# Two reorderings in a four-layer kernel: the choice of experts ahead of the first shared product, and another order in the head and period of the fused loop

## The reference, cut to what matters

```
L0 attention: 16 heads, 4 kv heads, rope, causal softmax
L0 experts:   scores = softmax(t @ gate_w.T); top 2 of 16 experts (inner width 176), weighted
              y = sum of w_e * (silu(t@w1) * (t@w3)) @ w2;  z = the same with the shared weights (width 352)
L1 ssm:       zxbcdt = x @ W_in; causal conv over 4 taps, silu; dt = softplus(dt + bias); dA = exp(dt * A)
              h = h*dA + dt*x*B;  y = h.C + D*x;  y = y * silu(gate)
              y = y * rsqrt(mean(y*y) + eps) * norm_w;  out = y @ W_out
L1 experts:   sigmoid scores, top 8 of 16 (width 128), normalised, scale 2.5, plus 2 shared experts
```

## Time and profile before

| what | value |
|---|---|
| median of 3 runs | 1957.74 us |
| lowest and highest | 1949.46, 1965.22 us |
| the profiled execution, its run | 1958.08 us |
| its span, first to last instruction | 1956.4 us |
| TensorE busy (matmuls) | 1837.6 us, 94% |
| VectorE busy | 1265.4 us, 65% |
| ScalarE busy | 768.6 us, 39% |
| GpSimd busy | 424.6 us, 22% |
| mean granted TensorE clock | 0.962 of full |

### The profile page before, as it was taken

How to read it: one execution, slowest core, us unless ns; L and a number is a source line. 1 busy time by engine, 2 the same in 40 slices (tenths; PEclk the granted TensorE clock), 3 DMA queues, 4 the chain that set the end, 5 groups by cost and what they waited for, 6 DMA issues and landing times.

```text
span 1956.4 us, 33621 instructions
## 1 busy us (share of the span) xinstructions
PE 1837.6 (94%) x9986; PEld 1417.0 (72%) x9987; DVE 1265.4 (65%) x3638; ACT 768.6 (39%) x1483; POOL 424.6 (22%) x708
## 2 busy tenths in 40 slices
PE   5999999969989999777999999999999999999998
PEld 3566666547766666555888888888888888888886
DVE  3577677545432222377777877887787778777843
ACT  1466666543223333343433343344333433433321
POOL 1244334331854444300110010011001100110000
PEclk9899999879989999887999999999999999999999
DMA  9900000001332333342112201220222022112210
GB/s 357 223 6 1 0 0 1 1 1 39 116 106 92 92 94 95 118 155 81 49 39 87 82 28 64 87 81 6 87 87 75 12 86 82 52 40 71 66 49 11
DMA packets 92119, 137.87 MB, mean 70 GB/s; under 512 B 18548, under 2 KB 76148, under 8 KB 91508
## 3 DMA queue, kind: packets, MB, share of 16 engines
q1 hardware_dynamic: 85108, 117.83, 18.9%
q0 software_dynamic: 6912, 18.92, 2.7%
HBM read 98.51 MB, written 38.22 MB: 70 GB/s over the span
## 4 chain that ended last, share of the span: by engine, by line
PE 43%; issue 38%; DVE 8%; POOL 7%; ACT 2%; DMA 1%; DVEq 0%; SPq 0%; POOLq 0%; ACTq 0%
PE bank L610 6%; PE bank L184 5%; PE bank L1311 4%; PE bank L631 4%; POOL sorted_in L858 3%; PE bank L1376 3%; PE bank L1269 2%; PE bank L193 2%; PE bank L1317 2%; PE bank L1299 2%; PE bank L1404 2%; PE bank L621 1%; PE bank L1362 1%; PE bank L539 1%; PE bank L1279 1%
## 5 line engine op out<-in xcount | busy, mean ns | idle before, releaser
L184 PE MATMUL bank<-moe_xT,up_w 128*128 128x256 f32 x2304 | 547.9, 381 | 0.0
L184 PEld LDWEIGHTS bank<-moe_xT,up_w 128*128 128x128 f32 x2304 | 439.8, 191 | 60.5 <-issue 0.2
L227 ACT ACTIVATE moe_silu<-bank 128x256 f32<-128x256 f32 x288 | 110.8, 385 | 576.3 <-PE bank L184 576.3
L193 PE MATMUL bank<-down_w,moe_hT 128*128 128x256 f32 x1152 | 303.9, 387 | 5.7 <-DVE moe_hT L294 2.9
L193 PEld LDWEIGHTS bank<-down_w,moe_hT 128*128 128x128 f32 x1152 | 207.1, 190 | 39.2 <-DVE moe_hT L294 8.2
L1557 DVE TENSOR_REDUCE q_slots<-bank 128x4 f32<-128x1024 f32 (+1 forms) x96 | 117.7, 1226 | 82.1 <-PE bank L1311 81.6
L1462 ACT ACTIVATE probs<-bank 128x1024 f32<-128x1024 f32 x96 | 98.2, 1023 | 100.6 <-PE bank L1317 100.6
L830 DVE TENSOR_TENSOR moe_h<-moe_silu,bank 128x176 f32<-128x176 f32 x80 | 27.0, 338 | 140.2 <-issue 83.2
L610 PE MATMUL bank<-up_w,moe_xT 128*128 x320 | 116.8, 488 | 0.7 <-ACT moe_xT L676 0.6
L1311 PE MATMUL bank<-kT,qT 16*128 16x256 f32 (+1 forms) x1024 | 115.2, 353 | 0.0
L293 DVE TENSOR_TENSOR moe_silu<-moe_silu,up_w 128x256 f32<-128x256 f32 x192 | 81.2, 423 | 51.7 <-ACT moe_silu L227 42.3
(11 more groups left out here) (309 smaller groups left out, 3257.9 us busy)
## 6 DMA issues: line engine op xcount, KB each, us to landing
up_w<-comb_rows SPq DMA_DIRECT2D x32, 768.0 KB, 5.2
m<-decay_rows SPq DMA_DIRECT2D x16, 1024.0 KB, 5.0
comb_got<-results SPq DMA_DIRECT2D x16, 768.0 KB, 7.7
moe_rows<-sorted_in SPq DMA_DIRECT2D x80, 128.5 KB
sorted_in<-zero SPq DMA_DIRECT2D x10, 1024.0 KB, 10.0
down_w<-comb_rows SPq DMA_DIRECT2D x16, 512.0 KB, 8.5
up_w<-in_up SPq DMA_DIRECT2D x2, 3168.0 KB, 15.2
up_w<-in_up SPq DMA_DIRECT2D x2, 2304.0 KB, 12.0
```

The lines of the kernel that those rows point to most:

```text
L184: last = mm(k.bank[:, UP_BANK + i % 3, half * S:(half + 1) * S], m.w_up[:, c, at + half * m.inter:at + (half + 1) * m.inter], m.xT[:, par, ...
L193: last = mm(k.bank[:, SUM_BANK, j * D:(j + 1) * D], m.hT[:, i % 3, j * P:(j + 1) * P], m.w_down[:, m.expert(i), :], start=(i == 0 and j == ...
L227: nc.scalar.activation(m.silu[:, i % 3, :], k.bank[:, UP_BANK + i % 3, 0:S], ACT.Silu).then_inc(m.silu_ready, 1)
```

## The change

**Shared stage.** Piece 0 of the choice goes ahead of the first transposes, pieces 1 to 3 ahead of the first up product, the others each some places earlier (piece 14 stays); the two rank products go from (1, 1) and (2, 1) to (0, 2) and (1, 2). The scatters start at (2, 2) instead of (3, 0).

**Scaling of `w_out`.** It moves from the start of the fused loop to VectorE's queue right behind the last shared step.

**Late steps.** ScalarE's Silu is cut from `l_up` as a step of its own, `l_silu`. In the head, for sequence b, the up products go behind `turn_dt`, the Silus behind the decays, the products `l_h` behind conv 2 and conv 3; `turn_dA`, `decay_out`, `decay_in` go ahead of the gates.

**Period.** In `THEN`, `table` 0, `one_plus`, `table` 1, `conv` 3 and `dt` 1 of the next sequence go from step 8 to step 9, behind `post` 0; step 8 keeps `out` and `conv` 2.

```diff
@@ -386,17 +386,21 @@
 
 
 CHOSEN = 12
-CHOICE = {(0, 0): (0,), (0, 1): (1, 2, 3), (0, 2): (4, 5, 6, 7), (1, 2): (8, 9), (2, 0): (10,), (2, 2): (11, 12), (3, 0): (13,),
-          (4, 0): (14,)}
-RANKS = {(1, 1): 0, (2, 1): 1}
-SCATTERS_FROM = 3
+AT_ONCE = (1, 2, 3)
+CHOICE = {(0, 0): (4, 5), (0, 1): (6, 7), (1, 0): (8,), (1, 1): (9, 10), (2, 0): (11, 12), (2, 1): (13,), (4, 0): (14,)}
+RANKS = {(0, 2): 0, (1, 2): 1}
+SCATTERS_FROM = (2, 2)
 EARLY = 14
 
 
 def shared_steps(chunks):
     yield "norm", 0, 0
+    yield "choose", 0, 0
     yield "turn_x", 0, 0
-    places = chunks * (EARLY - SCATTERS_FROM)
+    for n in AT_ONCE:
+        yield "choose", n, 0
+    first = chunks * SCATTERS_FROM[0] + SCATTERS_FROM[1]
+    places = chunks * EARLY - first
     tile = 0
     for t in range(EARLY):
         for c in range(chunks):
@@ -411,7 +415,7 @@
                 yield "turn_x", t + 1, 0
             for n in CHOICE.get((t, c), ()):
                 yield "choose", n, 0
-            place = chunks * (t - SCATTERS_FROM) + c + 1
+            place = chunks * t + c + 1 - first
             while place > 0 and tile < -(-TILES * place // places):
                 yield "scatter", tile, 0
                 tile += 1
@@ -817,6 +821,7 @@
     for what in shared_steps(m.shared_chunks):
         shared(*what)
 
+    scale_w_out(k, m.ssm, dve)
     seen = [0]
 
     def block(what, b, row):
@@ -903,7 +908,7 @@
     go_through(m.blocks, sp, block)
 
 
-LATE_STEPS = ("l_norm", "l_turn", "l_up", "l_h", "l_down", "l_end")
+LATE_STEPS = ("l_norm", "l_turn", "l_up", "l_silu", "l_h", "l_down", "l_end")
 
 
 class Late:
@@ -966,7 +971,7 @@
         if what == "l_turn":
             act.wait_ge(s.xT_full, m.turns + n + 1)
             nc.scalar.copy(moe.xT[:, t % 2].rearrange("p c t -> p (c t)"), k.bank[:, SUM_BANK, :]).then_inc(s.xT_ready, 1)
-        if what == "l_up":
+        if what == "l_silu":
             w = s.wide(c)
             act.wait_ge(s.up_full, m.up(t, c) + 1)
             if n > 0:
@@ -2027,6 +2032,13 @@
     return step
 
 
+def scale_w_out(k, m, dve):
+    dve.wait_ge(m.loaded, m.LOADS)
+    for f in range(FT):
+        last = k.nc.vector.tensor_scalar(m.w_out[:, f, :], m.w_out[:, f, :], m.norm_w[:, f:f + 1], None, ALU.mult)
+    last.then_inc(m.w_out_ready, 1)
+
+
 def ssm_vector(k, m, combine, dve, chain):
     nc = k.nc
     v = nc.vector
@@ -2160,10 +2172,6 @@
     link(v.memset(m.feat_bc[:, 0:TAPS - 1], 0.0))
     dve.wait_ge(m.loaded, m.LOADS)
 
-    for f in range(FT):
-        last = ts(m.w_out[:, f, :], m.w_out[:, f, :], m.norm_w[:, f:f + 1], None, ALU.mult)
-    last.then_inc(m.w_out_ready, 1)
-
     ts(m.a_lim[:], m.a_log[:], 88.0, None, ALU.min).then_inc(m.log_ready, 1)
     dve.wait_ge(m.tables, 2)
     link(ts(m.neg_a[:], m.pos_a[:], -1.0, None, ALU.mult))
@@ -2310,8 +2318,8 @@
         ((1, "turn_dt", 0), (0, "ymm", 1), (0, "square", 0), (1, "dt", 0), (1, "conv", 0), (-2, "m_post", 1)),
         ((1, "gate", 0), (0, "gating", 1), (2, "c_sum", 0)),
         ((1, "gate", 1), (0, "square", 1), (1, "conv", 1), (-2, "store", 0)),
-        ((0, "out", 0), (1, "table", 0), (1, "one_plus", 0), (1, "table", 1), (1, "conv", 2), (1, "dt", 1), (1, "conv", 3)),
-        ((0, "post", 0),),
+        ((0, "out", 0), (1, "conv", 2)),
+        ((0, "post", 0), (1, "table", 0), (1, "one_plus", 0), (1, "table", 1), (1, "conv", 3), (1, "dt", 1)),
         ((0, "post", 1), (1, "silu", 0), (2, "c_sum", 1)),
         ((1, "turn_c", 0), (0, "m_norm", 0)),
         ((1, "turn_c", 1), (0, "m_norm", 1), (1, "dt", 2), (2, "c_norm", 0)),
@@ -2339,15 +2347,16 @@
     def head(self):
         a, b = range(EARLY, B)
         yield "c_fetch", 0, 0, 0
-        for what, t, i in (("l_norm", a, 0), ("l_turn", a, 0), ("l_up", a, 0), ("c_sum", 0, 0), ("l_up", a, 1), ("c_sum", 0, 1),
-                           ("l_up", a, 2), ("l_h", a, 0), ("c_norm", 0, 0), ("l_h", a, 1), ("c_fetch", 1, 0),
-                           ("experts", 0, 0), ("norm", 0, 0), ("l_h", a, 2), ("l_norm", b, 0), ("norm", 0, 1),
-                           ("l_down", a, 0), ("turn_x", 0, 0), ("l_turn", b, 0), ("feat", 0, 0), ("l_up", b, 0), ("feat", 0, 1),
-                           ("l_h", b, 0), ("l_up", b, 1), ("bcdt", 0, 0), ("l_h", b, 1), ("turn_dt", 0, 0),
-                           ("dt", 0, 0), ("table", 0, 0), ("conv", 0, 0), ("one_plus", 0, 0), ("table", 0, 1), ("l_up", b, 2),
+        for what, t, i in (("l_norm", a, 0), ("l_turn", a, 0), ("l_up", a, 0), ("l_silu", a, 0), ("c_sum", 0, 0), ("l_up", a, 1),
+                           ("l_silu", a, 1), ("c_sum", 0, 1), ("l_up", a, 2), ("l_silu", a, 2), ("l_h", a, 0), ("c_norm", 0, 0),
+                           ("l_h", a, 1), ("c_fetch", 1, 0), ("experts", 0, 0), ("norm", 0, 0), ("l_h", a, 2), ("l_norm", b, 0),
+                           ("norm", 0, 1), ("l_down", a, 0), ("turn_x", 0, 0), ("l_turn", b, 0), ("feat", 0, 0), ("feat", 0, 1),
+                           ("bcdt", 0, 0), ("turn_dt", 0, 0), ("l_up", b, 0), ("l_up", b, 1), ("l_up", b, 2),
+                           ("dt", 0, 0), ("table", 0, 0), ("conv", 0, 0), ("one_plus", 0, 0), ("table", 0, 1),
                            ("dt", 0, 1), ("conv", 0, 1), ("dt", 0, 2), ("table", 0, 2),
-                           ("gate", 0, 0), ("conv", 0, 2), ("gate", 0, 1), ("turn_dA", 0, 0), ("decay_out", 0, 0), ("l_h", b, 2), ("conv", 0, 3),
-                           ("silu", 0, 0), ("decay_in", 0, 0), ("l_down", b, 0), ("c_sum", 1, 0), ("c_sum", 1, 1),
+                           ("turn_dA", 0, 0), ("decay_out", 0, 0), ("decay_in", 0, 0), ("l_silu", b, 0), ("l_silu", b, 1),
+                           ("gate", 0, 0), ("conv", 0, 2), ("l_silu", b, 2), ("l_h", b, 0), ("gate", 0, 1), ("conv", 0, 3),
+                           ("l_h", b, 1), ("silu", 0, 0), ("l_h", b, 2), ("c_sum", 1, 0), ("l_down", b, 0), ("c_sum", 1, 1),
                            ("c_norm", 1, 0), ("turn_c", 0, 0), ("turn_c", 0, 1),
                            ("norm", 1, 0), ("norm", 1, 1), ("turn_x", 1, 0), ("xdt", 0, 0)):
             yield what, t, t % 2, i
@@ -2474,6 +2483,7 @@
         comb_rows = nc.dram_tensor("comb_rows", (2, E, S), F32, kind="Internal").ap()
         second = Moe(k, 128, 2.5, up_w, down_w, gate1, [(moe1_loaded, 80)], comb_rows)
         attention, tail = Attention(k, a, gate0, first), Tail(k, Combine(k, results), Ssm(k, a), second, Late(k, first, second))
+        first.ssm = tail.ssm
         layers = [attention, first, tail]
         tail.weights(sb)
 
```

## The result

The changed kernel took 1983.89 us (median of 6 runs, 1980.3 to 1994.3), the kernel before 1956.55 us beside it: ratio 1.0137, 95% interval 1.0109 to 1.0164, so 27 us slower (21 to 32). Timed again later beside other runs of before it was 1978.40 against 1960.61 us, 1.0096 (1.0073 to 1.0118). Both intervals lie on the slower side; their middle is +23 us. The forecast was 1980.4 us.

A forecast was written before the change was run, and what follows sets the result against it. TensorE was taken to bound the loop's full periods (940.0 of 946 us busy), GpSimd the shared stage. 30.4 - 4.0 - 1.2 - 0.55 - 1.95 = +22.7 us gave 1980.4 us; own range 1973 to 1988, 8 in 10 1964 to 1999.

The forecast's parts named there:

- The size of the stall: Full periods: ScalarE's table detour behind step 9's Silu delays TensorE's `turn_c` by 2.17 us, 14 times, 30.4 us.
- the 0.48 us that TensorE waited for product 10 is not given back: Full periods: TensorE's 0.48 us wait stays despite the stall, since VectorE's own order moves by as much.
- My lower bound: Full periods: with the 0.48 us given back in every period, the loss is 14 x 1.69 = 23.7 us.
- Rival (c): Full periods: TensorE's clock falls to half after each stall, 1.29 us a period, 18 us: 1998 us; chance 0.12.
- my signs of being wrong: TensorE's busy share stays 99%, first scatter less than 2 us sooner, or matmuls behind the stalls at half clock.
- (a): Full periods: the loop hides the detour and the change does what it says, 1950 us; chance 0.12.
- (b): Full periods: half of the stall is hidden as VectorE's waits shrink, 1.1 us a period, 1965 us; chance 0.14.
- (d): Full periods: each table change costs more than its load, 3.8 us a period, +54 us, 2034 us; chance 0.02.
- Rival (e): Shared stage: rank waits cost TensorE what the scatters gain, stage at 0, 1984 us; chance counted within the forecast's own range.
- From there the pace of 3.00 us holds: Shared stage: after scatter 4, starting 3.9 us sooner, GpSimd's scatters keep 3.00 us each.
- GpSimd remains the bound: Shared stage: TensorE keeps 7 us idle after the rank waits, so GpSimd sets the end, 4.0 us sooner.
- Moved work: Gains from `w_out` scaling moved, 1.2 us; the head, 0.55 us; and the first period, 1.95 us.

## Why the prediction was right, and where it was not

**Which work sets the end, and the mechanism: right.** The loop had 6 us of idle TensorE time to give and much to lose. The loss sits ahead of `turn_c`, released by the conv's Silu, 14 times, and the loop's edit alone gives all of it.

**The size of the stall: 2.17 forecast, 2.08 measured**, the handover from the conv's Silu to `turn_c` having shrunk from 0.19 to 0.12 us. My step "the 0.48 us that TensorE waited for product 10 is not given back" failed: that wait was in 6 of 14 periods only (2.9 us in all, which made those periods 0.36 us longer), and behind the stall it is gone. My lower bound, which gave it back in all 14, was too low for the same reason: I had read one period. So 14 x 2.08 - 6 x 0.36 = 27.0 us, and with half clock behind two stalls, 1.0 us each, 29.0 (28.9 measured) in place of 30.4. The half clock was no term of my sum, and without it the sum would have been 2 us further off.

**Rival (c), the clock.** It was worked out for every period, +1.29 us each. It came in 2 of 14. One such fall makes an up product 1.69 us longer, of which VectorE, late itself, would have taken 0.67 anyway. The rival's mechanism is real, and it was one of my signs of being wrong; it came more often the longer the gap: none of 14 behind 0.40 us, 5 of 42 behind 1.92, 10 of 14 behind 3.44 us. The gap's length is not all of it, since both traces of the changed kernel have it in the same two periods.

**Rivals (a), (b) and (d).** Nothing hides the detour, and half of the stall is not hidden. For (d), three or four loads in a row show 0.02 us between a load and what follows, and the kernel with one load more per period lost nothing by it. The Trainium skill's figure for a switch, on "ScalarE: Activation LUTs", section What ACT_TABLE_LOAD costs (1283 ns and a drain of 1380 ns), agrees with these rows in its first part; the drain is seen in none of them, though ScalarE had no spare time there that could have hidden it. Rival (e) has the first trace's number for the stage, about 0, but not its cause: the two waits for the ranks came out as forecast, 1.8 us together.

**The shared stage: the failed step.** The early part held: waits for the ranks of 0.66 and 1.13 us (0.7 and 1.2 forecast), the first scatter 5.0 us sooner (4.1). So did scatter 4, 3.4 us sooner (3.9). What failed is the sentence behind it, "From there the pace of 3.00 us holds". From the first scatter to the last it took 93.2 to 95.4 us in the four traces of the old order and 96.0 to 100.9 us in the seven of the new, 3.9 us more on average. GpSimd started early and ran out of filled buffers: its waits behind the first scatter were 0.6, 1.3, 2.6 and 3.0 us in the old order and 4.1 to 8.6 us in the new. They have three sources. Piece 14 costs 1.89 us in all seven, behind 0.6 us that the old order has too. The place that the formula leaves empty costs 0.2 to 1.9 us. Single scatters that land late, 3.4 to 4.9 us from issue to refill instead of 2.6 to 2.8, cost up to 1.8 us each; both orders have them, the trace of the kernel before none, and they are a good part of what makes two traces differ. The empty place had to be read off the code: the old formula spreads 32 scatters over 33 places and leaves the last one empty, the new one spreads them over 34 and leaves one in the middle and the last one empty, so in both orders the last scatter stands at place (13, 1) of TensorE's order. I had the skipped place only in the lower end of my range.

The reason that I gave, that GpSimd remains the bound, is half right. A scatter takes GpSimd 2.9 us. TensorE needs 2.7 us for a place where nothing holds it (8.2 us for three places in four tiles running, in the second trace of the changed kernel); that its 42 up products between 443.0 and 568.2 us in the kernel before are 3.0 us apart on average includes its waits for VectorE. So GpSimd is the slower one, but by so little that a hold-up of TensorE decides as well which of the two is waited for. At the stage's end the two come close together. In nine of the 14 traces, the first of the changed kernel and that of the kernel before among them, the fetch followed the store of TensorE's last result by 0.5 us. In the other five it followed by 0.6 to 1.4 us, and in the three of these whose landings the trace has, the last scatter had landed less than 0.1 us earlier. I had worked the fetch out from the scatters alone. A lead of 5 us left 0.9 us, give or take 2, in the traces and 2.4, give or take 3, in the times; the traces exclude my 4.0 us, the times do not. How much of the lead each of these takes from the time stays open: the one run with piece 14 behind the scatters and without the empty place kept it in the trace and showed nothing of it in the times, and no run moved the empty place alone.

**Moved work: right.** -1.2, -0.5 and -2.05 us against -1.2, -0.55 and -1.95.

**The sum.** That 1980.4 us came within 4 us of the first timing and within 2 of the second is partly luck: in the trace the shared stage was 4.9 us worse than forecast, part of it by the disturbance at its end, the attention happened to be 2.0 us slower, and the loop 1.5 us better. The ratios of the parts (0.9962 and 1.0137) are the sounder test, -7.4 and +26.8 us, and they stand near the forecast's -5.7 and +28.5 us. The ends of my forecast's own range, 1973 and 1988 us, do not follow from its terms: the lower bounds give 1971.7 us and the upper ones 1982.9 us.

## What to carry to other kernels

Work on an engine with little to do is only free where it stands: before moving a detour, look what that engine releases next and how much time that handover has. Where two engines keep nearly the same pace, an earlier start of one is worth only what reaches the end: count the places, and look whether the last piece of work has moved at all. And when a period is 99% busy, the last per cent can still be had, from the follower that is late: two steps reordered so that ready instructions fill its wait were worth more here (13.7 us) than all helpful parts of the change together (7.4 us).

## What the runs showed of the hardware

A VectorE instruction stood still beside GpSimd's addition. From the kernel with the loop's edit alone:

```profile
885.98 1.26 POOL L2190 TENSOR_TENSOR down_w<-down_w 128x512 f32<-128x512 f32 x1 [24.52 <-ACT down_w L2025]
886.01 1.52 DVE L2090 SCALAR_TENSOR_TENSOR conv_bc<-feat_bc,taps_bc,conv_bc 72x256 f32<-72x256 f32 x1
```

It otherwise takes 0.47 us; here 1.52, ending 0.29 us behind GpSimd's end. In the first period of the changed kernel it met two conv instructions, of 1.52 and 0.94 us beside the additions from 881.58 to 883.71 us, so that `conv` 2 or 3 took 3.19 us for its four where it takes 1.67; it hid behind the wait for the output product. It stands in the traces of all kernels with steps 8 and 9 in another order but the one with the detour cut in two, and in none with the old order; I had counted `conv` 2 and 3 at their usual length there. The Trainium skill says, on "SBUF — State Buffer", section SBUF: two separate sides, that GpSimd and a VectorE operation with two inputs from SBUF share a port pair that one of them holds for its whole instruction; these rows agree.

The clock is the other thing: whether TensorE falls to 1.2 GHz behind a gap of 1.92 or 3.44 us is neither sure nor excluded by the gap's length alone, and the same code (the shared stage alone, traced twice) ran its first period in 60.1 us at a mean clock of 0.86 and in 63.1 us at 0.82.
